# Messages of the sheaves scattered as three bfloat16 pieces in a graph network on one Trainium2 core

## What is computed

```python
def gcn_conv(h, W, b):                       # layer 0, twice; h is 64 wide when summed
    h = h @ W
    agg = jax.ops.segment_sum(h[src] * norm[:, None], dst, num_segments=n)
aggregated = jax.ops.segment_sum(x[src], dst, num_segments=num_nodes)      # layer 1
...
m = jax.nn.relu(h[src] + edge_attr)          # layer 2, five times
agg = jax.ops.segment_sum(m, dst, num_segments=n)
```

## Time and profile before

| | us |
|---|---|
| median of three runs | 9178.54 |
| the profiled execution | 9176.64 |
| its span in the trace | 9174.8 |
| first fetch to last sum_up of the first edge call | 2989 to 3602 |

### The profile page before, as it was taken

How to read it: one execution, slowest core, us unless ns; L and a number is a source line. 1 busy time by engine, 2 the same in 40 slices (tenths; PEclk the granted TensorE clock), 3 DMA queues, 4 the chain that set the end, 5 groups by cost and what they waited for, 6 DMA issues and landing times. The chain is left out here.

```text
span 9174.8 us, 256266 instructions
## 1 busy us (share of the span) xinstructions
PE 6695.5 (73%) x61749; PEld 5700.8 (62%) x61755; DVE 5579.0 (61%) x14982; ACT 4878.7 (53%) x13233; POOL 5804.0 (63%) x5857
## 2 busy tenths in 40 slices
PE   5547676878980798798898798798556665566664
PEld 1545555657970797797797797797445554455554
DVE  6865555555550666666666666666556667466667
ACT  3013334435440665665665665665566674466664
POOL 0566557757757774774774774774577774677773
PEclk8558888988995899899899899899777888778787
DMA  1235553435533775785784784774466673566663
GB/s 40 62 110 160 157 155 101 120 80 168 146 81 108 229 240 142 234 241 143 232 241 138 233 241 140 235 241 141 148 181 192 190 204 98 153 189 190 190 197 98
DMA packets 1221610, 1511.32 MB, mean 165 GB/s; under 512 B 206525, under 2 KB 806113, under 8 KB 1205014
## 3 DMA queue, kind: packets, MB, share of 16 engines
q1 hardware_dynamic: 1013494, 1055.75, 37.0%
q0 software_dynamic: 207712, 450.99, 19.9%
HBM read 1276.37 MB, written 229.67 MB: 164 GB/s over the span
## 5 line engine op out<-in xcount | busy, mean ns | idle before, releaser
L1988 POOL DMA_INDIRECT rings<-rows_key,pick x2682 | 2616.9, 976 | 1321.2 <-issue 746.2
L1245 POOL DMA_INDIRECT bigDEF<-rows_key_value,idx x1664 | 1646.9, 990 | 690.2 <-issue 656.8
L2117 PE MATMUL wide<-bigDEF,bigC 128*128 128x128 bf16 (+2 forms) x32256 | 1832.1, 215 | 340.6 <-DVE bigC L2203 148.3
L2117 PEld LDWEIGHTS wide<-bigDEF,bigC 128*128 128x128 bf16 x32256 | 1681.5, 100 | 508.8 <-issue 454.0
L2228 DVE TENSOR_TENSOR bigDEF<-bigDEF,part 128x128 f32 (+1 forms) x3576 | 1014.3, 284 | 996.5 <-PE part L2082 385.9
L2082 PE MATMUL part<-rings 128*128 128x128 f32 (+1 forms) x7152 | 1098.8, 293 | 564.6 <-ACT rings L2016 419.5
L2082 PEld LDWEIGHTS part<-rings 128*128 128x128 f32 (+1 forms) x7152 | 938.5, 187 | 635.9 <-issue 573.9
L2001 ACT COPY pick<-pairs 128x3 int32 (+1 forms) x1192 | 222.0, 189 | 1935.9 <-PE part L2082 1660.0
L2008 ACT ACTIVATE rings<-iota,pairs 128x128 f32<-128x128 f32 x3576 | 1173.2, 391 | 27.1 <-PE part L2082 21.8
L1988 POOL DMA_INDIRECT rings<-rows_hidden,pick x894 | 863.9, 966 | 457.9 <-issue 241.1
L2139 PE MATMUL lump<-bigDEF,bigC 128*128 128x256 f32 x3840 | 936.8, 388 | 20.5 <-DVE bigDEF L2189 20.3
(11 more groups left out here) (425 smaller groups left out, 10233.1 us busy)
## 6 DMA issues: line engine op xcount, KB each, us to landing
bigC<-sheaf_hots SPq DMA_DIRECT2D x1152, 256.0 KB
rings<-in_attr SPq DMA_DIRECT2D x2235, 64.0 KB
bigC<-sheaf_attr SPq DMA_DIRECT2D x120, 1024.0 KB
walk_value<-bigDEF SPq DMA_DIRECT2D x416, 256.0 KB
rings<-walk_value SPq DMA_DIRECT2D x416, 256.0 KB
rings<-sheaf_steps SPq DMA_DIRECT2D x192, 256.0 KB
sheaf_hots<-bigC SPq DMA_DIRECT2D x192, 256.0 KB
bigB<-sheaf_hots SPq DMA_DIRECT2D x192, 256.0 KB
```

The lines of the kernel that those rows point to most:

```text
L1245: e.indirect_dma_start(gbuf[:, g, r, :], None, table, bass.IndirectOffsetOnAxis(ap=c.idx[:, g, r:r + 1], axis=0)).then_inc(c.gathered[g].s ...
L1988: e.indirect_dma_start(gbuf[:, draw(n), r, 0:width], None, table, bass.IndirectOffsetOnAxis(ap=c.pick[:, draw(n), r:r + 1], axis=0)).then_ ...
L2117: last = e.matmul(to, hot, terms, start=x < LOT and x % batch == 0 and j == 2, stop=x >= MARCH - LOT, skip_group_check=True)
```

## The change

The messages of a sheaf are no longer struck in fp32. Each batch of `room.msg` is split into three bfloat16 pieces (`room.cuts`), whose sum is the message to nearly fp32 precision. `top` on ACT takes the place of `clean` and writes the first piece (with Relu in an edge call, as a copy in the others, which had no clean); `cut` on DVE subtracts it from the message (and applies the Relu in an edge call); `halve` on ACT writes the second piece, and `pare` on DVE the third. `strike` multiplies the three pieces with marks in bfloat16, made from an iota of 16-bit integers, and adds them up in the same PSUM tile. The new operations have places of their own in the queues of ACT and DVE.

```diff
-    r.marks = ring.rearrange("p (a x) -> p a x", x=SPAN)
+    r.marks = ring[:, 0:free].bitcast(BF16).rearrange("p (a x) -> p a x", x=SPAN)
...
+    r.cuts = [t.bitcast(BF16).rearrange("p (j a x) -> p j a x", j=3, x=width) for t in cuts]
...
             def load_sheaf(i, h):
-                _hold(e, c.struck, lots(i, h, 0) - batches, c.tick_sp)
+                _hold(e, c.pared, lots(i, h, 0) - batches, c.tick_sp)
...
-            def clean(i, h, b):
-                x = room.msg[h][:, b * batch:(b + 1) * batch, :]
+            def top(i, h, b):
                 _hold(e, c.drained, lots(i, h, b) + 1, c.tick_act)
-                e.activation(x, x, ACT.Relu).then_inc(c.cleaned.sem, 1)
+                _hold(e, c.struck, lots(i, h, b) + (1 - batches), c.tick_act)
+                e.activation(room.cuts[b][:, 0, :, :], rows_of(h, b), ACT.Relu if edge else ACT.Copy
+                             ).then_inc(c.topped.sem, 1)
+
+            def halve(i, h, b):
+                _hold(e, c.cut, lots(i, h, b) + 1, c.tick_act)
+                e.activation(room.cuts[b][:, 1, :, :], rows_of(h, b), ACT.Copy).then_inc(c.halved.sem, 1)
...
                     if edge:
                         relu(i, n)
+                    if exists(*earlier(i, h)):
+                        for b in {1: (0,), 2: (1,), 3: (2,), 4: (3,)}.get(m, ()):
+                            halve(*earlier(i, h), b)
+                        for b in {0: (0, 1), 1: (2,), 2: (3,)}.get(m, ()):
+                            top(*earlier(i, h), b)
                     ahead(i, n)
-                    if edge and m < 3 and exists(*earlier(i, h)):
-                        for b in ((0, 1), (2,), (3,))[m]:
-                            clean(*earlier(i, h), b)
...
             def strike(i, h, b):
                 _hold(e, c.marked, tiles(i, h, (b + 1) * batch), c.tick_pe)
-                _hold(e, c.cleaned if edge else c.drained, lots(i, h, b) + 1, c.tick_pe)
+                _hold(e, c.pared, lots(i, h, b) + 1, c.tick_pe)
...
-                    last = e.matmul(lump[0:width, h, 0:SPAN], room.msg[h][:, a, :], room.marks[:, a % 8, :],
-                                    start=a == 0, stop=a == LOT - 1)
+                    for j in (2, 1, 0):
+                        last = e.matmul(lump[0:width, h, 0:SPAN], room.cuts[b][:, j, a - b * batch, :],
+                                        room.marks[:, a % 8, :], start=a == 0 and j == 2, stop=a == LOT - 1 and j == 0)
...
-                    e.tensor_scalar(room.marks[:, a % 8, :], c.wide_iota[:, :],
+                    e.tensor_scalar(room.marks[:, a % 8, :], c.short_iota[:, :],
...
+            def cut(i, h, b):
+                x = rows_of(h, b)
+                _hold(e, c.topped, lots(i, h, b) + 1, c.tick_dve)
+                if edge:
+                    e.scalar_tensor_tensor(x, x, 0.0, room.cuts[b][:, 0, :, :], ALU.max, ALU.subtract
+                                           ).then_inc(c.cut.sem, 1)
+                else:
+                    e.tensor_tensor(x, x, room.cuts[b][:, 0, :, :], ALU.subtract).then_inc(c.cut.sem, 1)
+
+            def pare(i, h, b):
+                _hold(e, c.halved, lots(i, h, b) + 1, c.tick_dve)
+                e.tensor_tensor(room.cuts[b][:, 2, :, :], rows_of(h, b), room.cuts[b][:, 1, :, :], ALU.subtract
+                                ).then_inc(c.pared.sem, 1)
...
-                    if m in (1, 2, 4) and exists(*earlier(i, h)):
-                        mark(*earlier(i, h), (None, 0, 1, None, 2)[m])
+                    if exists(*earlier(i, h)):
+                        for b in {1: (0,), 2: (1,), 3: (2,), 4: (3,)}.get(m, ()):
+                            cut(*earlier(i, h), b)
+                        for b in {2: (0,), 3: (1,), 4: (2,), 5: (3,)}.get(m, ()):
+                            pare(*earlier(i, h), b)
+                        for b in {1: (0,), 2: (1,), 4: (2,)}.get(m, ()):
+                            mark(*earlier(i, h), b)
...
             mark(final, 0, batches - 1)
+            for b in range(batches):
+                cut(final, 1, b)
             sum_up(final, 0, LOOSE * BUNCH)
             for b in range(batches):
+                pare(final, 1, b)
                 mark(final, 1, b)
             sum_up(final, 1, LOOSE * BUNCH)
```

More of the change, by code:

```diff
@@ L53 @@
 assert MARCH == LEGS * LEG and LEGS == 8 and LOT == 2 * LEG and HELD == 4
-assert (DRAWS + 2 * DEEP) * BUNCH <= 3 * RING * GROUP
+assert (DRAWS + 2 * DEEP) * BUNCH + 3 * GROUP // 2 <= 3 * RING * GROUP
 BLOCK_STEP = 3 * HID * 2
@@ L141, in _setup @@
     c.wide_iota = sb("iota", [P, SPAN])
+    c.short_iota = sb("short_iota", [P, SPAN], I16)
     c.iota = c.wide_iota[:, 0:P]
@@ L210, in _setup @@
     c.drained = gate("drained")
-    c.cleaned = gate("cleaned")
     c.struck = gate("struck")
+    c.topped = gate("topped")
+    c.cut = gate("cut")
+    c.halved = gate("halved")
+    c.pared = gate("pared")
     c.lumped = gate("lumped")
@@ L667, in _ @@
             step(lambda: e.tensor_scalar(tri, c.iota[:, :], c.node[:, 0:1], None, ALU.is_ge))
+            step(lambda: e.tensor_copy(c.short_iota[:, :], c.wide_iota[:, :]))
             e.wait_ge(c.moved.sem, c.moved.at(48))
@@ L1799, in _room @@
     r.hots = spare[:, 2 * msg:2 * msg + 2048].bitcast(BF16).rearrange("p (k x) -> p k x", k=HELD)
-    ring = left[:, 0:2048] if width == D else spare[:, 2 * msg + 2048:2 * msg + 4096]
-    r.marks = ring.rearrange("p (a x) -> p a x", x=SPAN)
+    free = 2 * GROUP * SPAN // 2
+    piece = 3 * GROUP * width // 2
+    ring = left if width == D else spare[:, 2 * msg + 2048:2 * msg + 4096]
+    r.marks = ring[:, 0:free].bitcast(BF16).rearrange("p (a x) -> p a x", x=SPAN)
     if width == D:
-        r.stage = [left[:, 2048 + k * size:2048 + (k + 1) * size] for k in range(2)]
-        r.stage += [left[:, k * size:(k + 1) * size] for k in range(2)]
+        r.stage = [left[:, k * size:(k + 1) * size] for k in range(4)]
+        cuts = [left[:, free + k * piece:free + (k + 1) * piece] for k in range(3)]
+        cuts.append(c.rings[:, 3 * RING * GROUP * P - piece:3 * RING * GROUP * P])
     else:
         r.stage = [left[:, k * size:(k + 1) * size] for k in range(4)]
+        cuts = [left[:, k * piece:(k + 1) * piece] for k in range(4)]
+    r.cuts = [t.bitcast(BF16).rearrange("p (j a x) -> p j a x", j=3, x=width) for t in cuts]
     tile, at = BUNCH * P, DRAWS * BUNCH * P
@@ L1881, in piece, with rows_of @@
             "p (a j f) -> p a j f", j=3, f=width)
+    def rows_of(h, b):
+        return room.msg[h][:, b * batch:(b + 1) * batch, :]
     def staged(t):
@@ L2066, in _ @@
                 half(final, h)
-            if edge:
-                for b in range(batches):
-                    clean(final, 1, b)
+            for b in range(batches):
+                top(final, 1, b)
+            for b in range(batches):
+                halve(final, 1, b)
         @block.tensor
@@ L2196, in drain @@
                 else:
-                    _hold(e, c.struck, lots(i, h, 0) - batches, c.tick_dve)
+                    _hold(e, c.pared, lots(i, h, 0) - batches, c.tick_dve)
                 for b in range(batches):
@@ L2296, in _mixed @@
         c.message.passed(LOOSE)
-        c.cleaned.passed(SHEAVES * batches)
         for g in c.sheaf:
@@ L2300, in _mixed @@
     c.marked.passed(QUEUE)
-    for g in (c.drained, c.struck):
+    for g in (c.drained, c.struck, c.topped, c.cut, c.halved, c.pared):
         g.passed(SHEAVES * batches)
```

## The result

The kernel after takes 9442.53 us (9439.33 to 9451.86) beside 9178.83 us for the kernel before on the same chip: a ratio of 1.029, with a 95% interval from 1.0272 to 1.0307. It is 264 us slower, where 124 were forecast, and lies above the forecast's whole range, which ended at 9420. The span of the profiled execution is 9439.0 us.

A forecast was written before the change was run, and what follows sets the result against it. It took GpSimd's indirect fetches to fill the period in seven calls. Terms: edge calls 106, third 21, second 5, fresh 0, ends -8, sum +124 us on the profiled execution, giving 9302 us; range 9185 to 9420.

The forecast's parts named there:

- GpSimd's fetches bound seven of eight calls: All but the fresh call: fetches plus 0.30 us behind each fill the period, 22.4 us a sheaf, 22.9 in edge calls.
- Strikes 1.34 us, cut and pare 0.69, marks cheaper: Operation prices: strike 1.34 us on TensorE, cut 0.685 and pare 0.692 on DVE, each mark 0.07 less.
- The stretch: Two-SBUF-input cut and pare lengthen GpSimd's fetches, 0.88 us a sheaf: +106 us edge calls, +21 third, +5 second.
- The walk of one sheaf: Edge calls, from leg 7's end: next leg 7 ends at T+23.3, hidden by 0.5 us under GpSimd's 23.8.
- The pick is covered: ACT's pick comes some 5 us later behind top, but GpSimd wants it some 9 us later: no cost.
- The rival, the round as the bound: ACT, DVE and TensorE's round becomes the bound if waits grow by over 0.5 us: 9425 us, chance 0.17.
- the prediction's own sign for it: Profile after: GpSimd's idle before a fetch exceeding 0.30 us behind ACT's pick would show the round as bound.
- Ends of calls: After the last drain: about 14.4 us, -1 us for each of 8 calls, -8 us (bounds -25, +10).
- The fresh call, forecast at 0: First call, where make_hots waits for step rows: new operations' cost against savings taken as 0, bounds -20 and +20 us.

The follow-up runs named there:

- e4: e1 with cut, halve and pare taken out and strikes of four bfloat16 products (one piece, bfloat16 precision): 9098.57 us, ratio 0.9914.
- e3: Kernel after with pick and select ahead of halve and top on ACT, and sum_up at place 5 on DVE: 9265.67 us, ratio 1.0093.
- e8: Kernel before plus eight DVE maximum operations a sheaf (128x384) ahead of the adds, both inputs in SBUF: 9465.0 us, ratio 1.0335.
- e9: Kernel before plus the same eight DVE operations a sheaf as e8, but with the second input in PSUM: 9444.27 us, ratio 1.031.
- e7: e1 without the third piece: no pare, strikes of eight products: 9215.65 us, ratio 1.0061.
- e2: Kernel after with sum_up moved on DVE from place 2 to place 5: 9345.19 us, ratio 1.018.
- e1: Kernel after with ACT's pick and select moved ahead of halve and top at each place: 9277.91 us, ratio 1.0104.
- e10: Kernel before with sum_up moved on DVE from place 2 to place 5, nothing else: 9143.53 us, ratio 0.9981.

## Why the prediction was right in its direction and wrong in its size

**GpSimd's fetches bound seven of eight calls: held for the kernel before.** e4 shows it best: much of TensorE's and DVE's work taken away moved neither steady period. For the kernel after it held in the second and the third call and failed in the five edge calls.

**Strikes 1.34 us, cut and pare 0.69, marks cheaper: held.** Measured 1.31, 0.686, 0.683; a mark went from 0.373 to 0.299 us in the groups, 0.074 less where 0.07 was put.

**The stretch: held in size.** Third call: forecast 0.88 us a sheaf, measured 400/309 x 18 - 400/321 x 18 = 0.87. Its fetches took 19.8 us longer from first to last start (560.2, then 580.0); 21 were forecast. Second call: 4.7 us, 5 forecast. In the edge calls it was 0.6 in after, where GpSimd had slack anyway, and 0.8 in e3, where it had none. e8 and e9 give the cause by itself. The account by number and length of the operations, 0.11 us for each, held in the third call (e7) and not in the edge calls of e7, where four cost as much as eight.

**The walk of one sheaf: this is the step that failed.** It had 20.5 us of TensorE and 2.85 of waiting, and leg 7 ended at T+23.3, "hidden, by 0.5 us". In the timeline leg 7 ends at T+24.9. The work is as forecast: 8 x 1.34 + 6 x 0.72 + 4 x 1.31 = 20.3 us. The waits are 4.6, and they lie elsewhere: scatters 1, 2 and 4 wait 0.2, 0.1 and 1.6 us, where 0.7, 0.75 and 1.4 were forecast, leg 0 waits 1.2 for the drain and leg 4 starts 0.9 late. What decides is when scatter 4 starts. By the walk's own terms (three strikes, five legs, four scatters and the 2.85 of waiting) that is T+16.4; in the trace it is T+17.95, so all of the 1.6 us is lost by then, and TensorE was ready earlier, so neither the drain nor leg 4 is the cause. The relu that it waits for comes late because `cut` of batch 2 does: 2.93 us lie between the end of that `cut` (T+15.0) and scatter 4, so the walk must have had it end near T+13.5 (an estimate from these rows). The walk's DVE had no stall around sum_up; the trace has 0.85 + 0.44 = 1.3 us there, right before that `cut`. The kernel before shows them too, so the walk could have had them:

```profile
3314.26 0.42 DVE L2210 TENSOR_TENSOR bigDEF<-bigDEF,lump 128x256 f32 x1 [1.54 <-issue]
3315.13 1.15 DVE L2228 TENSOR_TENSOR bigDEF<-bigDEF,part 128x128 f32 x3 [0.45 <-DVE bigDEF L2210]
```

So the walk was 1.6 us short, three times its margin. e2 takes the stall away (97 us back, 69 of them in the edge calls) and e1 takes the pick and the select out of the same chain (165 us back).

**"The pick is covered": it fell with the walk.** Once the round sets the period, GpSimd catches up with the picks, however far ahead they are ordered. Its wait for them is the sign of the round, not a loss of its own.

**The rival, the round as the bound, is what happened.** It had 24.8 us a sheaf and 9425 us; the trace has 24.9 in this sheaf (25.2 by the count of fetches), and the time was 9442.5. Its condition, waits grown together by over 0.5 us, was met with 4.6 in place of 2.85, and so was the prediction's own sign for it, GpSimd idle for more than 0.30 us behind ACT's pick. With 0.17 it had too small a chance for a margin of 0.5 us in a walk of 23. The range did not even hold it: its upper end, 9420, was said to take in most of the new round and lies below the round's own 9425.

**Ends of calls, -8 us forecast: the part after the drain missed, more was won elsewhere.** The edge call's last drain to last sum_up took 15.7 us, 15.4 before, and 14.4 forecast, though the terms that the prediction lists make 13.4. In the trace `top` of the last batch waits 2.4 us for a strike, because its buffer still holds the pieces of the sheaf before. But the second and the third call lost 4.7 and 19.8 us up to the last fetch and only 0 and 14 in all. So 5 to 6 us came back behind the last fetch, where TensorE has work left; that the shorter strikes did it is argued, and cannot be all: e10 has the fp32 strikes of before, and behind the last fetch of these two calls it too is 4 to 5 us shorter. In the fresh call 13 us were lost up to the last fetch and 9 came back behind it. The fresh call, forecast at 0 with 20 either way, lost 4.

Summed: the edge calls' 243 us (forecast 106 less 5), third 14 (20), second 0 (4), fresh 4 (-1). The whole error is in the edge calls.

## What to carry to other kernels

When a change puts operations into a chain over three queues, the chain's own period must be read off the trace with its idle times, the stalls marked "issue" among them; a margin of half a microsecond is none in a walk that leaves such stalls out. A load of words for addresses shows in no engine's busy time; the sequencer's rows have it. Moving two short operations from the link of a chain to a place beside it (e1) was worth more (165 us) than the whole stretch of the fetches that the forecast was about (132). Before giving work to VectorE beside GpSimd's indirect DMAs, see whether it can read one of its inputs from PSUM. That saves the stretch of the fetches alone: e9 was still 285 us slower than before, only 21 us better than e8.

## What the runs showed of the hardware

- A vector operation with two SBUF inputs delays fetches and the same one with an input in PSUM does not: 967 and 946 ns in the third call, with operations of 566 and 552 ns.
- In the third call the price of one such operation at 384 elements was 0.047 us, little more than half of the 0.083 that the joins had seemed to cost. In the kernel after, at 512 elements, it was 0.87/8 = 0.11. In edge calls the number does not fix it: 1013 ns a fetch with four more (e7), 992 with eight more (e1).
- Loading words for addresses holds a sequencer: on DVE 1.41 us for six words (L1103) and 0.31 for one (L1110), on TensorE 1.11 for the addresses of two legs (L2143). sum_up, behind such loads at place 2, had 0.9 us of idle time ahead of it in the edge calls after (14.3 us, x16), 1.8 in the fresh call before, and 0.3 there at place 5.
